# A two-layer attention kernel: in the first layer the inverted row sums reach the channels by two transfers through memory, and the turn of the maxima moves between the two projections

## The chip, the cores and the metric

One core of a Trainium2 chip runs the kernel. The metric is the device time of one execution in microseconds (us). A difference of under 1% of it is taken as no change.

## The reference

The input x is 32 images of 16 x 16 tokens with 256 channels. Two layers follow one another, each a residual around attention on the group-normalised input (`_gn`: 32 groups of 8 channels, statistics per image).

```
x = x + _L0_conv_ref(_gn(x), ...)      # windowed cosine attention, shifted windows of 8 x 8
x = x + _L1_conv_ref(_gn(x), ...)      # masked attention, 8 heads look back and 8 look ahead
```

The change is in the first layer alone. There an image is rolled by (-4, -4) and cut into 4 windows of 64 tokens; with 16 heads of 16 channels:

```
qn = q / max(|q|, 1e-12);  kn = k / max(|k|, 1e-12)
logits = qn @ kn^T * exp(min(logit_scale, log 100)) + 16 * sigmoid(bias)   # masked across the roll
scores = softmax(logits, axis=-1)                                          # 64 keys per query
o = scores @ v;   z = o @ Wo^T + bo                                        # back to 256 channels
```

The softmax divides by a sum for each head and each query. The kernel weighs the values first and divides the 256 channels of the result afterwards, so each inverted sum is needed in the 16 rows (channels) of its head.

## The kernel before, in words

**Layout.** In the first layer channels lie on the 128 partitions in 2 tiles (`o`), tokens along the free axis: 256 for an image. Scores lie with keys of two heads on 2 x 64 partitions, and 4 quarters (`r`, QUADS) in 4 PSUM banks, `psG`. Sums go to `psE`, four quarters of 32 rows each. `psA` has three banks: two for the projections of queries and keys, one for the values and the weighed values.

**Order of the work.** Each engine runs its own list of stages, written out by hand, in `pipeline`: in step s every stage of the list runs for image s + lag, in the order of the list. Steps -6 to 3 and 26 to 32 are written out, the steps between are a loop of two steps in a pass. Engines meet only at semaphores (`wait`), and each engine's list is executed in order. `wait_alone` is a wait followed by a `nop` inside the loop.

**TensorE's step** (list at L467): `scores` of image s (L339, L346), `project_v` of s+1 (L382), `output` of s-1 (L396), `bounds` of s+1 (L363, L370), `turn` of s+2 (L407), `sums` of s (L417), `weigh` of s (L431), `project` half 0 of s+3 (L443), `groups` of s+4 (L458), `project` half 1 of s+3 (L443 again), `turn_c` of s+1 (L450), and `spread_sums` of s (L465): one 128 x 128 by 128 x 512 product in float32, recorded as two matmuls, that copies each inverted sum into the 16 rows of its head. `output` waits for the divided heads, `scores` for the turned maxima (`c_out`), `turn` for the unit queries and keys (`qkn_done`), `sums` for both halves of `add_bias`.

**VectorE's step** (list at L740): `add_bias` half 0 (L634), `unit_qk` (L714, two), `add_bias` half 1, `take_max` (L707, two), `invert_sums` (L618), `spread_blocks` (L623), `stats_next` (L722), `stats_first` (L729 to L737), `variances` (L647 to L653), `norms` (L641, twice, each after one `square`), `outputs` (L613), `seeds` (L663 to L669) and `roots` (L675 to L699). `spread_blocks` writes the inverse sums, masked by block, as a 128 x 512 operand `rdx` for `spread_sums`; `outputs` multiplies the result in `psE` with the weighed values in `ot`.

**ScalarE's step** (list at L565): the two halves of `exponent` (L522), `copy_v`, `copy_z`, `normalize`, `copy_qk`, `copy_o` (L547, fills `ot`), `square` half 0 and half 1 (L506), and `copy_c` (L552), which turns the maxima in `psG` into the bfloat16 operand that `scores` of the next step uses.

**GpSimd** adds the residual. **SyncE** has one stage in the loop, `load` (L286): the 256 KB image s+6 into `X`, once the statistics of image s+4 are done.

The second layer is not touched.

Of the kernel before, what the change touches and what calls it, by code (L numbers as in the profile page):

```python
# [30 lines left out]
P = 128  # L31
# [149 lines left out]
def layer0(nc, ctx, images, xr, given, X, stats2, probs, xh, stack, ident, gavg, A, G, E):  # L181
    def sb(name, shape, dt=F32):
        return ctx.enter_context(nc.sbuf_tensor(name, shape, dt))

    def sem(name):
        return ctx.enter_context(nc.semaphore(name))
# [5 lines left out]
    qkn = probs[0][:, 3072:4096].rearrange("p (t c) -> p t c", t=TT)  # L192
    rdx = probs[0][:, 4096:4608]
    sel = probs[0][:, 4608:4864].rearrange("p (n j) -> p n j", j=COL)
    spread = probs[0][:, 4864:4992]
    aqf = probs[0][:, 4992:5248]
    zb = probs[1][:, 2048:2560].rearrange("p (c t) -> p c t", c=CT)
    wo = probs[1][:, 3072:3584].rearrange("p (c o) -> p c o", c=CT)
# [30 lines left out]
    own = sb("own0", [P, 2])  # L229
    half_of = sb("half_of", [P, 2])  # L230
    slot_of = sb("slot_of", [P, 4])
    block_of = sb("block_of", [P, 8])
    group_of = sb("group_of", [P, QUADS, 2])
    region_keys = sb("region_keys", [P, 4, WTOK], BF16)
    region_queries = sb("region_queries", [P, TOKENS], BF16)
    pick = sb("pick0", [P, 4, WTOK], BF16)
# [2 lines left out]


    x_in = [sem(f"x_in{k}") for k in range(2)]
    pv_done, proj_qk, proj_v, max_ready, s_ready, z_ready, turned, c_turned, g_ready, spread_done = (
        sem(n) for n in ("pv_done", "proj_qk", "proj_v", "max_ready", "s_ready", "z_ready", "turned",
                         "c_turned", "g_ready", "spread_done"))
    squared, exp_done, z_out, qk_out, c_out, xh_done, v_out = (
        sem(n) for n in ("squared", "exp_done", "z_out", "qk_out", "c_out", "xh_done", "v_out"))
    r_done, o_done, sum_done, gn_chain, rs_ready, max_done, qkn_done, x1_done, stats = (
        sem(n) for n in ("r_done", "o_done", "sum_done", "gn_chain", "rs_ready", "max_done", "qkn_done",
                         "x1_done", "stats"))
    newton, biased, rdx_done, sums_done, o_out = (sem(n) for n in ("newton", "biased", "rdx_done", "sums_done", "o_out"))  # L250
    LAGS = (-1, 6)
    NEWTON = 9
    CUBIC = math.sqrt(0.375)
# [14 lines left out]
           (scale, given["scale0"]), (bv, given["bv0"]), (bo, given["bo0"]), (wo, given["wo0"])]  # L268
    others = [(gavg, given["gavg"]), (wqk, given["wqk0"]), (ident, given["ident"]), (wv, given["wv0"])]
    REGIONS = 2 * QUADS  # L270
    MADE = 12
    TABLE_STEP = -2

    with nc.Block() as block:
        @block.sync
        def _(sp):
            for group, done in ((net, c_net), (others, c_in)):
                for dst, src in group:
                    sp.dma_start(dst if isinstance(dst, bass.AP) else dst[:], src).then_inc(done, 16)
            sp.wait_ge(z_in, 2)  # L280
            for r in range(QUADS):
                rows = slice(r * COL + SLOTS, r * COL + SLOTS + MASKS)
                sp.dma_start(region_keys[rows, :, :], given["aux"][0:MASKS, 1, 0:4, win(WINDOWS - 1)]).then_inc(region_in, 16)
                sp.dma_start(region_queries[rows, :], given["aux"][0:MASKS, 0, 0, :]).then_inc(region_in, 16)

            def load(i):  # L286

                wait_alone(sp, stats, i.plus(-2).count(4, 1))
                src = xr.rearrange("(c p) i t -> p c i t", p=P)[:, :, bass.ds(i.index(), 1), :]
                sp.dma_start(X[:, bass.ds(i.index(1), 1), :, :].rearrange("p i c t -> p c (i t)"),  # L290
                             src.rearrange("p c i t -> p c (i t)")).then_inc(x_in[i.k], 16)

            pipeline(sp, images, [(load, 6)], LAGS)

        @block.tensor
        def _(pe):
# [114 lines left out]
            def sums(i):  # L411

                wait(pe, biased, i.count(2))
                wait(pe, z_out, i.plus(-1).count(2))
                for n in range(8):
                    for r in range(QUADS):
                        last = nc.tensor.matmul(E[own_rows(r), 0:WTOK], sel[:, n, :], prob[i.k][:, r, n // WINDOWS, n % WINDOWS, :],  # L417
                                                start=(n == 0), stop=(n == 7), tile_position=(0, r * COL), skip_group_check=True)
                        if n == 7:
                            last.then_inc(sums_done, 1)  # L420
# [38 lines left out]
                                 bn[i.k][:, :, :].rearrange("p c (h s) -> p (c h) s", s=3)[:, :, 1:3],  # L459
                                 start=True, stop=True).then_inc(g_ready, 1)  # L460

            def spread_sums(i):

                wait(pe, rdx_done, i.count(1))
                nc.tensor.matmul(E[:, :], spread, rdx, start=True, stop=True).then_inc(spread_done, 1)  # L465

            pipeline(pe, images, [(scores, 0), (project_v, 1), (output, -1), (bounds, 1), (turn, 2), (sums, 0), (weigh, 0),  # L467
                                  (lambda i: project(i, 0), 3), (groups, 4), (lambda i: project(i, 1), 3), (turn_c, 1),
                                  (spread_sums, 0)], LAGS, once=(TABLE_STEP, prepare))

        @block.scalar
        def _(act):
# [81 lines left out]
            def normalize(i):  # L554
# [3 lines left out]
                for c in range(CT):  # L558
                    src = X[:, bass.ds(i.index(1), 1), c, :].rearrange("p i (t rr ww c) -> p (i t) rr ww c", t=TT, rr=WIN, ww=2)
                    dst = xh[i.k][:, c, :].rearrange("p (t ww rr c) -> p t rr ww c", t=TT, ww=2, rr=WIN)  # L560
                    for ww in range(2):
# [2 lines left out]

            pipeline(act, images, [(lambda i: exponent(i, 0), 0), (lambda i: exponent(i, 1), 0),  # L565
                                   (copy_v, 1), (copy_z, -1), (normalize, 3), (copy_qk, 2),
                                   (copy_o, 0), (lambda i: square(i, 0), 3), (lambda i: square(i, 1), 3), (copy_c, 1)], LAGS, once=(TABLE_STEP, finish_table))

        @block.vector
        def _(dve):  # L570
# [7 lines left out]
            def prepare():  # L578
                dve.wait_ge(c_in, 16 * len(others))
                dve.wait_ge(region_in, 16 * REGIONS)  # L580
                nc.vector.tensor_scalar(aqf, region_queries[:, :], -1.0, None, ALU.mult).then_inc(made, 1)
                unit = ident[:, :]
                nc.vector.reduce_sum(own[:, :], unit.rearrange("p (r e d) -> p e r d", e=2, d=DIM), AX_XY).then_inc(summed, 1)
                nc.vector.reduce_sum(half_of[:, :], unit.rearrange("p (e k) -> p e k", e=2), AX_X).then_inc(summed, 1)
                nc.vector.reduce_sum(slot_of[:, :], unit.rearrange("p (r j) -> p j r", j=COL)[:, 0:SLOTS, :],
                                     AX_X).then_inc(summed, 1)
                by_sum = unit.rearrange("p (r u e n) -> p u r e n", r=QUADS, u=2, e=2)[:, 0]
                nc.vector.reduce_sum(block_of[:, :], by_sum.rearrange("p r e n -> p n r e"), AX_XY).then_inc(summed, 1)
                nc.vector.reduce_sum(group_of[:, :, :], by_sum, AX_X).then_inc(summed, 1)
                dve.wait_ge(summed, 5)  # L590
                nc.vector.tensor_tensor(pick[:, :, :], region_keys[:, :, :], slot_of[:, :].unsqueeze(2).to_broadcast([P, SLOTS, WTOK]),
                                        ALU.add).then_inc(made, 1)
                nc.vector.tensor_copy(spread.rearrange("p (g d) -> p g d", d=DIM),
                                      group_of[:, :, :].rearrange("p r e -> p (r e)").unsqueeze(2)
                                      .to_broadcast([P, 8, DIM])).then_inc(made, 1)
                for n in range(8):
                    nc.vector.tensor_copy(sel[:, n, :].rearrange("p (u e n) -> p u e n", u=2, e=2)[:, :, :, n],
                                          half_of[:, :].unsqueeze(1).to_broadcast([P, 2, 2])).then_inc(made, 1)
                dve.wait_ge(p_cm, 1)
                nc.vector.tensor_copy(cm[:, :, :].rearrange("p t s -> p (t s)"), G[:, 512:768]).then_inc(made, 1)  # L600
                dve.wait_ge(made, MADE)

                dve.wait_ge(a_tab, 1)
                nc.vector.tensor_scalar(table, table, 1.0, None, ALU.add).then_inc(d_tab, 1)
                dve.wait_ge(d_tab, 1)
                nc.vector.reciprocal(table, table).then_inc(d_tab, 1)

            def outputs(i):

                wait(dve, spread_done, i.count(1))  # L610
                wait(dve, o_out, i.count(1))
                raw = ot[:, :, :].rearrange("p o t -> p (o t)")
                nc.vector.tensor_tensor(raw, E[:, :], raw, ALU.mult).then_inc(o_done, 1)  # L613

            def invert_sums(i):
                wait(dve, sums_done, i.count(QUADS))
                wait(dve, rdx_done, i.plus(-1).count(1))
                nc.vector.reciprocal(rd[:, :], E[:, 0:WTOK]).then_inc(r_done, 1)  # L618

            def spread_blocks(i):  # L620
                wait(dve, r_done, i.count(1))
                wait(dve, spread_done, i.plus(-1).count(1))
                nc.vector.tensor_tensor(rdx.rearrange("p (n q) -> p n q", q=WTOK), rd[:, :].unsqueeze(1).to_broadcast([P, 8, WTOK]),  # L623
                                        block_of[:, :].unsqueeze(2).to_broadcast([P, 8, WTOK]), ALU.mult).then_inc(rdx_done, 1)

            def add_bias(i, part):

# [97 lines left out]
            def stats_first(i):  # L725
                wait_alone(dve, x_in[i.k], i.dmas(1))
                wait_alone(dve, g_ready, i.plus(-2).count(1))
                for c in range(CT):
# [9 lines left out]
                                               op0=ALU.mult, op1=ALU.add).then_inc(stats, 1)  # L738

            pipeline(dve, images, [(lambda i: add_bias(i, 0), 0), (unit_qk, 2), (lambda i: add_bias(i, 1), 0), (lambda i: take_max(i, 0), 1), (lambda i: take_max(i, 1), 1),  # L740
                                   (invert_sums, 0), (spread_blocks, 0), (stats_next, -1), (stats_first, 5),
                                   (variances, 4), (lambda i: norms(i, 0), 3), (lambda i: norms(i, 1), 3), (outputs, 0),
                                   (seeds, 4, 1), (roots, 4, 1)], LAGS,
                     once=(TABLE_STEP, prepare))
# [544 lines left out]
```

## Time and profile before

| | |
|---|---|
| time, median of 3 runs | 1286.02 us (1282.92 to 1295.72) |
| the profiled execution's own time | 1287.98 us |
| its span | 1286.3 us |
| TensorE's granted clock, mean over the span | 0.975 |
| first layer, from the span's start to about | 565 us |
| TensorE matmuls busy | 1194.4 us (93%) |
| TensorE weight loads busy | 864.1 us (67%) |
| VectorE busy | 897.7 us (70%) |
| ScalarE busy | 610.9 us (47%) |
| GpSimd busy | 207.4 us (16%) |

How to read it: the times of the engines overlap, so they don't add up to the span. A busy share is an average over both layers; what one instruction is worth is read from the step in which it runs. The profile's span is 1.7 us shorter than the execution's time, and the execution is 2 us above the median of the runs.

### The profile page before, as it was taken

Reading aid. Unit: us, or ns where it says so; the run is one execution under the profiler, and the core shown is the slowest. Engines: PE = TensorE matmul, PEld = TensorE weight load, DVE = VectorE, ACT = ScalarE, POOL = GpSimd, SP = SyncE. Lnnn points to the kernel's source line nnn. Section 1 sums busy time; section 2 is a strip of 40 time slices with the busy share of each in tenths; the row PEclk is TensorE's granted clock in tenths of the full one; section 3 lists DMA queues with packets and bytes.
Section 4 is the critical chain, followed back from the end, with each engine's and each line's share of the span. In section 5 each row is a group of like instructions: output and inputs, shape, how many; then the busy total and the mean of one; then the engine's idle time right before and its main releaser. Section 6 shows DMA issues by size and latency. Waiting matters only on the chain.

```text
span 1286.3 us, 50697 instructions
## 1 busy us (share of the span) xinstructions
PE 1194.4 (93%) x21404; PEld 864.1 (67%) x21404; DVE 897.7 (70%) x1591; ACT 610.9 (47%) x1019; POOL 207.4 (16%) x271
## 2 busy tenths in 40 slices
PE   6789999999999999958999999999999999999983
PEld 2567777777677677736677776767777777767652
DVE  1488898798888888645576666767666666767643
ACT  2355565555555555512444444444444444445430
POOL 0001111111111111121222212212222212222120
PEclk9699999999999999989999999999999999999987
DMA  2000000000000000010232423333232323333233
GB/s 80 13 20 20 20 17 17 20 16 25 12 24 16 18 12 3 5 38 1 34 65 64 79 48 74 52 70 57 65 58 66 75 51 76 51 71 56 67 58 74
DMA packets 304632, 54.35 MB, mean 42 GB/s; under 512 B 270724, under 2 KB 303766, under 8 KB 304534
## 3 DMA queue, kind: packets, MB, share of 16 engines
q1 hardware_dynamic: 303480, 52.75, 19.9%
q8 instruction: 83, 1.36, 0.4%
q10 hardware_dynamic: 1056, 0.13, 0.1%
q14 instruction: 13, 0.11, 0.0%
HBM read 27.56 MB, written 25.17 MB: 41 GB/s over the span
## 4 chain that ended last, share of the span: by engine, by line
PE 45%; DVE 5%; issue 3%; ACT 1%; DMA 1%; SPq 0%; POOL 0%; POOLq 0%; DVEq 0%
PE psG L979 8%; PE psA L1042 7%; PE psG L1011 6%; PE psA L1056 5%; PE psG L1022 5%; PE psE L1090 5%; PE psA L1068 4%; DVE of L1189 3%; PE psG L994 2%; DVE sums L1184 2%; PE psE L1080 1%; ACT probs L1113 0%; SPq L947 0%; DVE cm L1165 0%; DMA scratch_heads<-ots 0%
## 5 line engine op out<-in xcount | busy, mean ns | idle before, releaser
L1165 DVE TENSOR_REDUCE cm<-psG 128x4 f32<-128x1024 f32 (+1 forms) x192 | 235.2, 1225 | 174.5 <-PE psG L1022 174.3
L1113 ACT ACTIVATE probs<-psG 128x1024 f32<-128x1024 f32 x192 | 196.5, 1023 | 240.5 <-PE psG L994 240.5
L1219 POOL TENSOR_SCALAR_AFFINE_SELECT probs<-probs 128x1024 f32<-128x1024 f32 x128 | 139.1, 1098 | 551.0 <-ACT probs L1113 551.0
L979 PE MATMUL psG<-stack 32*128 32x512 f32 (+1 forms) x1024 | 219.2, 525 | 6.3 <-ACT probs L1113 6.3
L1011 PE MATMUL psG<-stack 32*128 32x256 f32 (+1 forms) x2048 | 219.2, 341 | 4.1 <-DVE cm L1165 2.7
L1011 PEld LDWEIGHTS psG<-stack 32*128 32x128 f32 x2048 | 149.6, 185 | 10.8 <-DVE cm L1165 3.4
L764 POOL TENSOR_TENSOR X<-X,probs 128x96 f32 (+5 forms) x128 | 62.0, 515 | 499.2 <-ACT probs L529 499.2
L443 PE MATMUL psA<-probs,xh 128*128 128x512 f32 x256 | 130.5, 637 | 9.3 <-ACT xh L562 5.3
L1056 PE MATMUL psA<-xh,wqk 128*128 128x256 f32 x512 | 122.6, 383 | 5.7 <-DVE xh L1195 5.7
L979 PEld LDWEIGHTS psG<-stack 32*128 32x128 f32 x1024 | 82.8, 185 | 61.6 <-issue 54.3
L1184 DVE RECIPROCAL sums<-sums 128x128 f32<-128x128 f32 x128 | 115.7, 929 | 12.0 <-DMA sums<-scratch_heads 12.0
L1056 PEld LDWEIGHTS psA<-xh,wqk 128*128 128x128 f32 x512 | 93.3, 192 | 17.4 <-DVE xh L1195 6.4
L1042 PE MATMUL psA<-probs,va 128*32 128x256 f32 (+1 forms) x2048 | 97.8, 332 | 0.9 <-POOL probs L1219 0.9
L522 ACT ACTIVATE probs<-psG 128x1024 f32<-128x1024 f32 x64 | 62.0, 1021 | 76.1 <-PE psG L346 76.1
L634 DVE TENSOR_TENSOR probs<-probs,ebias 128x1024 f32<-128x1024 f32 x64 | 77.9, 1219 | 14.6 <-ACT probs L522 14.5
L1090 PE MATMUL psE<-of,wo 128*128 128x256 f32 x256 | 67.0, 407 | 21.7 <-DVE of L1189 20.5
L707 DVE TENSOR_REDUCE cm<-psG 128x16 f32<-128x1024 f32 x64 | 75.4, 1219 | 14.8 <-PE psG L370 13.9
L1042 PEld LDWEIGHTS psA<-probs,va 128*32 128x32 f32 x2048 | 57.8, 110 | 34.5 <-issue 11.7
L506 ACT ACTIVATE probs<-psA 128x512 f32<-128x512 f32 x64 | 38.2, 597 | 87.1 <-PE psA L443 83.0
L443 PEld LDWEIGHTS psA<-probs,xh 128*128 128x128 f32 x256 | 45.6, 198 | 45.6 <-issue 33.2
L994 PE MATMUL psG<-ct,pick 32*128 32x256 bf16 (+1 forms) x1024 | 74.4, 242 | 0.0
L1090 PEld LDWEIGHTS psE<-of,wo 128*128 128x128 f32 x256 | 48.2, 198 | 36.2 <-DVE of L1189 23.2
(132 smaller groups left out, 1925.5 us busy)
## 6 DMA issues: line engine op xcount, KB each, us to landing
scratch_heads<-ots SPq DMA_DIRECT2D x256, 64.0 KB, 3.6
X<-in_xr SPq DMA_DIRECT2D x32, 256.0 KB, 2.8
raw<-scratch_heads SPq DMA_DIRECT2D x32, 256.0 KB, 2.7
sums<-scratch_heads SPq DMA_DIRECT2D x32, 256.0 KB, 3.0
out<-X SPq DMA_DIRECT2D x32, 256.0 KB, 2.9
probs<-in_wqk SPq DMA_DIRECT2D x1, 512.0 KB, 4.0
wv<-in_wv SPq DMA_DIRECT2D x2, 256.0 KB, 4.2
wqk<-in_wqk SPq DMA_DIRECT2D x1, 512.0 KB, 4.0
```

What stands on the lines that cost most here:

```text
L443: last = nc.tensor.matmul(A[t][:], xh[i.k][:, c, t * P:(t + 1) * P], wqk[:, c, :], start=(c == 0), stop=(c == CT - 1))
L634: nc.vector.tensor_tensor(both, both, bias.unsqueeze(2).to_broadcast([P, 4, WINDOWS, WTOK]), ALU.mult).then_inc(biased, 1)
L979: nc.tensor.matmul(G[:, at:at + 2 * b.size].rearrange("p (e q) -> p e q", e=2), kt[i.k][own_rows(r), o, b.keys_of(o) * P:(b.keys_of(o) + 1 ...
L994: last = nc.tensor.matmul(G[:, at:at + b.size], pick[own_rows(r), e, :], ct[o][own_rows(r), b.queries(o)], start=False, stop=True, skip_gr ...
L1011: nc.tensor.matmul(G[:, at:at + b.size], qm[i.k][own_rows(r), o, e, b.queries_of(o) * P:(b.queries_of(o) + 1) * P], kt[i.k][own_rows(r), o ...
L1042: last = nc.tensor.matmul(A[0 if o else 2][COL * c:COL * (c + 1), to:to + b.size], va[i.k][:, b.keys_of(o), TILE_HEADS * o + 2 * r + e, :] ...
L1056: last = nc.tensor.matmul(A[o][:, n * TOKENS:(n + 1) * TOKENS], wqk[:, c, n * CH + o * P:n * CH + (o + 1) * P], xh[i.k][:, c, :], start=(c ...
L1090: last = nc.tensor.matmul(E[:, o * TOKENS:(o + 1) * TOKENS], wo[:, f, o * P:(o + 1) * P], of[:, f, :], start=(f == 0), stop=(f == CT - 1))
L1113: nc.scalar.activation(weights[:, b.weights_at:b.weights_at + 1024], G[:, 0:1024], ACT.Exp).then_inc(exp_done, 1)
L1165: nc.vector.reduce_max(slots, scores, AX_X).then_inc(max_done, 1)
L1184: nc.vector.reciprocal(piece, piece).then_inc(r_done, 1)
L1219: nc.gpsimd.affine_select(out=diagonal, in_=diagonal, compare_op=ALU.is_ge, fill=0.0, base=0, pattern=[[0, QUADS], [0, 2], [sign, P]], cha ...
```

## The change

`spread_sums`, `spread_blocks` and the two reductions and the copy that made their masks (`block_of`, `group_of`, `spread`) are gone. SyncE gets two stages after `load`: `put_inverses` writes the 128 x 64 inverses (32 KB) to one of two buffers in device memory, and `get_inverses`, once that transfer has landed, reads 8 rows of 512 numbers (2 KB) from there, each 16 times, into the 128 x 512 operand `rdx` (256 KB). `outputs` waits for this transfer and multiplies by `rdx` in place of `psE`. The order of the columns in `sel` is changed so that the wanted sums lie where `get_inverses` reads them. `invert_sums` waits for the previous `put`, and `sums` for the previous `invert_sums`. On TensorE `turn_c` moves ahead of the second half of `project`, on ScalarE `copy_c` ahead of the second `square`.

```diff
-    spread = probs[0][:, 4864:4992]
...
-    block_of = sb("block_of", [P, 8])
-    group_of = sb("group_of", [P, QUADS, 2])
+    inverses = nc.dram_tensor("inverses", [2, P, WTOK], F32).ap()
...
-            pipeline(sp, images, [(load, 6)], LAGS)
+            def put_inverses(i):
+                wait_alone(sp, r_done, i.count(1))
+                wait_alone(sp, got[i.k], i.plus(-2).dmas(1))
+                sp.dma_start(inverses[i.k], rd[:, :]).then_inc(put[i.k], 16)
+
+            def get_inverses(i):
+                wait_alone(sp, put[i.k], i.dmas(1))
+                wait_alone(sp, o_done, i.plus(-1).count(1))
+                by_head = inverses[i.k].rearrange("(g u n) q -> g u (n q)", u=2, n=8)[:, 0]
+                sp.dma_start(rdx, by_head.unsqueeze(1).to_broadcast([8, DIM, 512])).then_inc(got[i.k], 16)
+
+            pipeline(sp, images, [(load, 6), (put_inverses, 0), (get_inverses, 0)], LAGS)
...
                 wait(pe, z_out, i.plus(-1).count(2))
+                wait(pe, r_done, i.plus(-1).count(1))
...
-            def spread_sums(i):
-
-                wait(pe, rdx_done, i.count(1))
-                nc.tensor.matmul(E[:, :], spread, rdx, start=True, stop=True).then_inc(spread_done, 1)
-
...
-                                  (lambda i: project(i, 0), 3), (groups, 4), (lambda i: project(i, 1), 3), (turn_c, 1),
-                                  (spread_sums, 0)], LAGS, once=(TABLE_STEP, prepare))
+                                  (lambda i: project(i, 0), 3), (groups, 4), (turn_c, 1), (lambda i: project(i, 1), 3)], LAGS, once=(TABLE_STEP, prepare))
...
-                                   (copy_o, 0), (lambda i: square(i, 0), 3), (lambda i: square(i, 1), 3), (copy_c, 1)], LAGS, once=(TABLE_STEP, finish_table))
+                                   (copy_o, 0), (lambda i: square(i, 0), 3), (copy_c, 1), (lambda i: square(i, 1), 3)], LAGS, once=(TABLE_STEP, finish_table))
...
-                    nc.vector.tensor_copy(sel[:, n, :].rearrange("p (u e n) -> p u e n", u=2, e=2)[:, :, :, n],
+                    nc.vector.tensor_copy(sel[:, n, :].rearrange("p (e u n) -> p u e n", u=2, e=2)[:, :, :, n],
...
-                wait(dve, spread_done, i.count(1))
+                wait_alone(dve, got[i.k], i.dmas(1))
                 wait(dve, o_out, i.count(1))
                 raw = ot[:, :, :].rearrange("p o t -> p (o t)")
-                nc.vector.tensor_tensor(raw, E[:, :], raw, ALU.mult).then_inc(o_done, 1)
+                nc.vector.tensor_tensor(raw, rdx, raw, ALU.mult).then_inc(o_done, 1)

             def invert_sums(i):
                 wait(dve, sums_done, i.count(QUADS))
-                wait(dve, rdx_done, i.plus(-1).count(1))
+                wait_alone(dve, put[1 - i.k], i.plus(-1).dmas(1))
                 nc.vector.reciprocal(rd[:, :], E[:, 0:WTOK]).then_inc(r_done, 1)
-
-            def spread_blocks(i):
-                wait(dve, r_done, i.count(1))
-                wait(dve, spread_done, i.plus(-1).count(1))
-                nc.vector.tensor_tensor(rdx.rearrange("p (n q) -> p n q", q=WTOK), rd[:, :].unsqueeze(1).to_broadcast([P, 8, WTOK]),
-                                        block_of[:, :].unsqueeze(2).to_broadcast([P, 8, WTOK]), ALU.mult).then_inc(rdx_done, 1)
```

## Rows read from the trace of the kernel before

**Rows 1.** Busy time by stretch: start:end, length, engines, granted clock, DMA share, GB/s.
```profile
300.00:400.00 100.00, 96.74 (x2677) 71.73 (x2674) 86.23 (x207) 58.41 (x110) 12.78 (x28) 1.00 0.07 20
```

**Rows 2.** Timeline of one step on PE: start, length, line, operation, count.
```profile
305.85 0.38 PE L450 MATMUL psG<-ident,cm 128*128 128x128 f32 x2
306.06 1.02 PE L465 MATMUL psE<-probs 128*128 128x512 f32 x2
307.05 1.53 PE L339 MATMUL psG<-stack 32*64 32x64 f32 x124
...
314.02 1.09 PE L407 MATMUL psA<-ident,probs 128*128 128x128 f32 x8
315.04 1.10 PE L417 MATMUL psE<-probs 128*32 128x64 f32 x64
...
318.93 1.96 PE L443 MATMUL psA<-probs,xh 128*128 128x512 f32 x4
```

**Rows 3.** Timeline of the same stretch on ACT and DVE; idle time before in brackets.
```profile
306.05 0.60 ACT L506 ACTIVATE probs<-psA 128x512 f32<-128x512 f32 x1 [1.34 <-DVE rs L641]
306.68 0.69 DVE L641 TENSOR_REDUCE rs<-probs 128x32 f32<-128x512 f32 x1 [0.62 <-ACT probs L506]
307.28 0.68 DVE L613 TENSOR_TENSOR ot<-psE,ot 128x512 f32<-128x512 f32 x1
...
310.62 1.22 DVE L634 TENSOR_TENSOR probs<-probs,ebias 128x1024 f32<-128x1024 f32 x1
311.75 1.28 DVE L714 TENSOR_TENSOR probs<-psA,rs_y 128x512 f32<-128x512 f32 x2
312.95 1.22 DVE L634 TENSOR_TENSOR probs<-probs,ebias 128x1024 f32<-128x1024 f32 x1
314.26 2.36 DVE L707 TENSOR_REDUCE cm<-psG 128x16 f32<-128x1024 f32 x2
316.53 0.55 DVE L618 RECIPROCAL rd<-psE 128x64 f32<-128x64 f32 x1
317.12 0.69 DVE L623 TENSOR_TENSOR probs<-rd,block_of 128x512 f32<-128x512 f32 x1
317.73 0.75 DVE L722 BATCH_NORM_STATS2 stats<-X  x2
```

**Rows 4.** Timeline on PE: first and last of 28 steps, L465 in each.
```profile
88.56 1.02 PE L465 MATMUL psE<-probs 128*128 128x512 f32 x2
...
508.34 1.02 PE L465 MATMUL psE<-probs 128*128 128x512 f32 x2
```

**Rows 5.** DMA issues of the page: size, us from issue to landing (medians).
```profile
X<-in_xr SPq DMA_DIRECT2D x32, 256.0 KB, 2.8
...
out<-X SPq DMA_DIRECT2D x32, 256.0 KB, 2.9
```

**Rows 6.** DMA queue q1: packets, MB, share of 16 engines; the whole span, then 100 to 560 us.
```profile
q1 hardware_dynamic: 303480, 52.75, 19.9%
```
```profile
q1 hardware_dynamic: 6528, 6.29, 4.6%
```

**Rows 7.** The chain that ended last, in time: start, length, what.
```profile
1267.78 3.64 DMA scratch_heads<-ots
1271.42 0.02 issue
1271.44 0.36 SPq L955
```

**Rows 8.** The last steps of the first layer, timeline on DVE, then PE.
```profile
547.62 0.55 DVE L618 RECIPROCAL rd<-psE 128x64 f32<-128x64 f32 x1
...
556.78 0.56 DVE L618 RECIPROCAL rd<-psE 128x64 f32<-128x64 f32 x1 [1.30 <-PE psE L417]
...
559.28 0.69 DVE L613 TENSOR_TENSOR ot<-psE,ot 128x512 f32<-128x512 f32 x1 [0.56 <-PE psE L465]
```
```profile
551.90 2.05 PE L396 MATMUL psE<-ot,probs 128*128 128x128 f32 x16
...
555.53 1.10 PE L417 MATMUL psE<-probs 128*32 128x64 f32 x64 [1.58 <-DVE probs L634]
```

**Rows 9.** Busy time by stretch: around a long wait of PE inside `scores`.
```profile
228.00:231.00 3.00, 1.33 (x115) 1.19 (x110) 2.57 (x13) 0.00 (x0) 0.00 (x0) 1.00 0.00 0
231.00:236.00 5.00, 5.00 (x70) 4.47 (x49) 3.44 (x4) 3.12 (x4) 0.00 (x0) 0.66 0.01 3
```

More of the change, by code:

```diff
@@ L241, in layer0 @@
     x_in = [sem(f"x_in{k}") for k in range(2)]
[L242 removed]
+    pv_done, proj_qk, proj_v, max_ready, s_ready, z_ready, turned, c_turned, g_ready = (
         sem(n) for n in ("pv_done", "proj_qk", "proj_v", "max_ready", "s_ready", "z_ready", "turned",
[L244 removed]
+                         "c_turned", "g_ready"))
     squared, exp_done, z_out, qk_out, c_out, xh_done, v_out = (
@@ L249, in layer0 @@
                          "x1_done", "stats"))
-    newton, biased, rdx_done, sums_done, o_out = (sem(n) for n in ("newton", "biased", "rdx_done", "sums_done", "o_out"))
+    newton, biased, sums_done, o_out = (sem(n) for n in ("newton", "biased", "sums_done", "o_out"))
+    put, got = ([sem(f"{n}{k}") for k in range(2)] for n in ("put", "got"))
     LAGS = (-1, 6)
@@ L270, in layer0 @@
     REGIONS = 2 * QUADS
-    MADE = 12
+    MADE = 11
     TABLE_STEP = -2
@@ L586, in prepare @@
                                      AX_X).then_inc(summed, 1)
[L587 to L590, printed above, removed]
+                dve.wait_ge(summed, 3)
                 nc.vector.tensor_tensor(pick[:, :, :], region_keys[:, :, :], slot_of[:, :].unsqueeze(2).to_broadcast([P, SLOTS, WTOK]),
                                         ALU.add).then_inc(made, 1)
-                nc.vector.tensor_copy(spread.rearrange("p (g d) -> p g d", d=DIM),
-                                      group_of[:, :, :].rearrange("p r e -> p (r e)").unsqueeze(2)
-                                      .to_broadcast([P, 8, DIM])).then_inc(made, 1)
                 for n in range(8):
-                    nc.vector.tensor_copy(sel[:, n, :].rearrange("p (u e n) -> p u e n", u=2, e=2)[:, :, :, n],
+                    nc.vector.tensor_copy(sel[:, n, :].rearrange("p (e u n) -> p u e n", u=2, e=2)[:, :, :, n],
                                           half_of[:, :].unsqueeze(1).to_broadcast([P, 2, 2])).then_inc(made, 1)
@@ L740, in _ @@
             pipeline(dve, images, [(lambda i: add_bias(i, 0), 0), (unit_qk, 2), (lambda i: add_bias(i, 1), 0), (lambda i: take_max(i, 0), 1), (lambda i: take_max(i, 1), 1),
-                                   (invert_sums, 0), (spread_blocks, 0), (stats_next, -1), (stats_first, 5),
+                                   (invert_sums, 0), (stats_next, -1), (stats_first, 5),
                                    (variances, 4), (lambda i: norms(i, 0), 3), (lambda i: norms(i, 1), 3), (outputs, 0),
```

## The prediction

> **What bounds the kernel now.** I read the busy times by stretch first, to see which engine sets the first layer's pace. Between 300 and 400 us TensorE is busy 97% of the time at full clock and VectorE 86% [rows 1]: TensorE leads, VectorE is close behind. Then I read the timeline of one step, engine by engine. On TensorE there is no gap; `spread_sums` starts at 306.06 and `scores` of the next step at 307.05, so it takes 0.99 us of the step [rows 2]. On VectorE the only gap is 0.62 us before the second `norms`, which waits for the second `square`, and that for the second `project` [rows 3]. VectorE then has 7.5 us of work without a pause up to the end of `add_bias`. The 28 steps from 88.56 to 508.34 us take 419.78 us [rows 4]. 17 of their 27 gaps are 14.86 to 15.03 us, 14.93 on average; ten are longer because TensorE's sequencer stalls: 16.46, 15.45, 16.26, 18.76, 16.18, 17.30, 16.22, 17.39, 16.49 and 15.53, together 166.04.
>
> **The change part by part.** The sum is made against the profiled execution, 1288 us, 2 us above the median.
>
> *Removed on TensorE*: 0.99 us in each step. TensorE's own step would be 14.93 - 0.99 = 13.94 us. *Removed on VectorE*: `spread_blocks`, from 317.12 to 317.73, 0.6 us [rows 3]. The masks are made once, by three small instructions before the first step; I count nothing.
>
> *Moved*: `turn_c` costs 0.21 us (305.85 to 306.06) [rows 2] wherever it stands, and `groups` ahead of it already waits for both maxima, so it waits for nothing new. It makes the second `project`, and so the second `square`, 0.21 us later. In return `copy_c` runs under the second `project`, and `scores` can start at once. Its cover before was `spread_sums`.
>
> *The chain across the engines, if the transfers are hidden.* The second `project` ends at 306.01 (`square` starts at 306.05). `norms`, `outputs`, `seeds`, `roots`, `add_bias`, `unit_qk` and `add_bias` follow without a gap to 312.95 + 1.22 = 314.17, 8.16 us later [rows 3]. Before, `sums` started at 315.04 only because TensorE was busy. TensorE alone would now reach `sums` 7.99 us after the start of `scores` (307.05 to 315.04), or 7.8 us after the end of `project`, as pitches overlap by 0.16. So VectorE becomes what `sums` waits for: 8.16 + 0.04 for the semaphore. From `sums` to the end of the next second `project` it is 318.93 - 315.04 + 0.21 + 1.96 = 6.06 us [rows 2]. The step cannot be shorter than 14.26 us: of the 0.99 us only 0.67 can be had.
>
> *Added: the transfers.* `outputs` now waits for `rdx`, in VectorE's list, and behind it stand `seeds`, `roots`, `add_bias` and `unit_qk`, for which `turn`, `sums` and `normalize` wait. Call L the time from the end of the reciprocal to the start of `outputs`. The ring on VectorE is: end of `add_bias` (314.17) to the end of the reciprocal (316.53 + 0.55), 2.91; L; start of `outputs` to end of `add_bias` (307.28 to 314.17), 6.89 [rows 3]. Step = 9.80 + L. It is hidden up to L = 4.46, and equals today's 14.93 at L = 5.13.
>
> No row has these two transfers. A 256 KB image in 256 packets of 1 KB lands in 2.8 us, a 256 KB store in 2.9 [rows 5]. Between 100 and 560 us 24 image loads took 4.6% of 16 engines [rows 6]: 0.88 us on each engine for one load, 55 ns a packet. Over the whole span a packet has 174 bytes and takes 13.5 ns [rows 6]. The line through both is about 5 ns + 0.049 ns a byte (an estimate): 18 ns for a packet of 256 bytes, 105 ns for one of 2 KB. The `put` (128 packets of 256 bytes) takes 0.14 us on each engine, so 2.8 - 0.74 = 2.1 us; bounds 1.4 us (the same step again below it, for a store that is quick on a quiet queue) and 2.9 (the store as it stands). I take 2.1, the size taken off the nearest row. The `get` (128 packets of 2 KB) takes 0.84 us on each of 16 engines, then it lands in 2.8; if it runs on half of them 1.68, then in 3.6. Its source has an outer count of 8 (8 rows, each read 16 times) where the image's is 128, so it is likelier near the upper end; but 105 ns is a line drawn beyond its points, and larger packets may be cheaper. I take 3.3.
>
> The Trainium skill, "DMA: Bandwidth & Descriptors", section "Why a DMA increments its semaphore by 16 and not by 1", says that the number of engines is the largest up to 16 that divides the outermost count of both patterns. That would be 8 here, and L 0.3 us longer than I take; no row of before shows it.
>
> Handing over costs little: from landing to the next issue 0.02 us [rows 7]. With the register work and `nop` of `wait_alone` I take 0.05 + 0.1 + 0.05. L = 0.05 + 2.1 + 0.1 + 3.3 + 0.05 = 5.6, bounds 4.4 and 6.7. SyncE's queue: `load` of the next image is issued just behind the `get`, so it does not delay it, and lands a step before it is used. `sums` waits for a reciprocal a step old, `invert_sums` for a `put` long landed: nothing.
>
> *The sum.* Step = 9.80 + 5.6 = 15.40. The 17 even steps: 17 x (15.40 - 14.93) = +8.0. In the ten long ones TensorE's stall covers the ring, and they become the larger of 15.40 and the old one less 0.99: 15.47, 15.40, 15.40, 17.77, 15.40, 16.31, 15.40, 16.40, 15.50, 15.40 = 158.45, so -7.6. The layer's end has no work to cover L. For the last image the reciprocal ends at 557.34 and `outputs` starts at 559.28 [rows 8]: 1.94 becomes 5.6, +3.7. For the one before, 548.17 + 5.6 + 0.69 + 2.05 (`output`) = 556.5, and `sums`, queued behind it, stood at 555.53 [rows 8]: +1.0. Total +5.1: 1293 for the execution, **1291 us** against the median.
>
> **The rivals.**
>
> *A. The transfers become the bound (slower).* The place is `outputs` on VectorE. At put 2.9 and get 3.6, L = 6.7, step 16.50: +26.7, +0.2, and +6.9 at the end: +34, 1320. It costs over 13 us from L = 5.9 on (15.70: +13.1 - 5.7 + 5.3). For it: a `get` on half of the engines and `put` as taken give just this 5.9, +13, 1299. Against it: everything else on the queue is idle at that time.
>
> *B. The transfers are nearly hidden (faster).* `get` as an image load, 2.8, put 2.0: L = 5.0, step 14.80: -2.2 - 9.3 + 3.5 = -8, 1278. With L at 4.4 the chain across the engines holds, 14.26: -11.4 - 9.9 + 2.5 = -19, 1267. For it: equal bytes to the image's. Against it: the 8 rows, and two landings in a row need under 4.75 us for a gain of 1%.
>
> *C. The removed matmul was not what TensorE waited for.* It covered the sequencer's fetches at the loop's head; stalls appear in its place. TensorE has about 1.4 us of idle time in a step by then (15.40 - 13.94), which hides them: 1286 to 1293, within 1%.
>
> *D. The clock.* TensorE waits before `turn` and `sums`, these 1.4 us a step. After a wait of 1.67 us inside `scores` the granted clock fell to 0.66 of full speed for 5 us [rows 9], that is partly the lower of its two levels (1.2 GHz); that step took 18.76 us, and one with a like stall and no fall 17.30. If this came in every second step, 1.46 x 14 = 20 us, less what the wait on VectorE absorbs, some half: 1301. Against it: the step with 17.30 lies in the stretch that shows 1.00 [rows 1].
>
> **How the numbers follow.** Under 1%, 13 us, is what a measurement of this kernel can't tell from no change. Chances: forecast (L 5.1 to 5.9) 0.42, its own range 1281 to 1299; A beyond 5.9 0.27; B 0.23; C 0.03; D 0.05. Of B 0.19 is beyond -13 us, since the bounds of `put` are wide to the low side. Faster 0.19, within 1% 0.49, slower 0.32. The range leaves out the outer part of A and B: 1267 to 1310.
>
> **What would show it.** Right: no L465 and no L623; `outputs` on VectorE with idle time before it ended by the DMA of `rdx`, 1 us a step; `turn` on TensorE released by L714; even steps of 15.4 us, so longer than 14.93 although 1 us of TensorE's work is gone; `put` landing in about 2.1 and `get` in about 3.3 us; `scores` with no wait for `copy_c`. Wrong: a `get` at 2.8 or a put under 1.7 (steps below 14.9); landings above 6 us together; a granted clock under 1.00 in the even steps; long steps that don't shorten.

## The result, and the profile after

The changed kernel takes 1325.9 us (median of 4 runs, 1319.65 to 1328.93) against 1284.5 before: 1.032 times as long, 95% interval 1.026 to 1.038. The forecast was 1291, its range ended at 1310. The profiled execution took 1323.1 us, its span is 1321.3, 35.0 longer than before.

**Where it went.** From the first layer's last `output` to the end of the span it is 724 us before and 725 after. In the first layer, the 28 steps that took 419.8 us [rows 4] now take 443.2 between starts of `turn_c`, +23.4. From there to the end of the last `output` it is 12.4 us longer, and the start is 1.7 shorter. The median gap is 16.04 us; counted in the same way it was 14.98. TensorE's timeline, the first and last of 28:

```profile
86.66 0.42 PE L461 MATMUL psG<-ident,cm 128*128 128x128 f32 x2
...
529.88 0.41 PE L461 MATMUL psG<-ident,cm 128*128 128x128 f32 x2
```

One step of the changed kernel: VectorE, then SyncE's queue, then TensorE (start, length, line, operation, count, idle time before and what ended it). It answers to [rows 2, 3].

```profile
330.05 0.54 DVE L617 RECIPROCAL rd<-psE 128x64 f32<-128x64 f32 x1
...
334.60 0.69 DVE L634 TENSOR_REDUCE rs<-probs 128x32 f32<-128x512 f32 x1 [1.26 <-ACT probs L511]
336.48 0.69 DVE L612 TENSOR_TENSOR ot<-probs,ot 128x512 f32<-128x512 f32 x1 [1.19 <-DMA probs<-inverses]
```
```profile
330.73 0.35 SPq L295 DMA_DIRECT2D inverses<-rd  x1
332.33 0.62 SPq L301 DMA_DIRECT2D probs<-inverses  x1
333.67 0.39 SPq L289 DMA_DIRECT2D X<-in_xr  x1
```
```profile
342.71 1.09 PE L417 MATMUL psA<-ident,probs 128*128 128x128 f32 x8 [1.80 <-DVE probs L707]
```

Read it as the ring of the prediction. The reciprocal ends at 330.59. The `put` is issued 0.14 later, the `get` 1.60 after the `put`, and `outputs` starts 4.15 after the `get` was issued: L = 5.89 us here. In the loop's other steps it is 5.9 to 6.5, median 6.2, but for one of 9.14; the prediction took 5.6. VectorE is idle for 1.19 us, and TensorE, which had no gap before, waits 1.80 us before `turn` for the unit queries and keys. 9.80 + 6.2 = 16.0 us is the step.

The page's DMA issues (size, us from issue to landing; the `get` has no figure) answer to [rows 5]. The image's load, now issued behind the `get`, lands later too; no engine is seen to wait for it:

```profile
X<-in_xr SPq DMA_DIRECT2D x32, 256.0 KB, 3.5
...
inverses<-rd SPq DMA_DIRECT2D x32, 32.0 KB, 1.5
```

From the issue of the `get` to the start of `outputs` it is 4.4 us in the median of the loop's steps (4.1 to 4.7). The layer's last six `get`s have no image's load behind them and stand outside the loop, without the `nop` of `wait_alone`; there it is 3.8 to 4.1. The prediction held that the load does not delay the `get`. What of the difference is the load's, no run separates.

**The clock** falls after some of TensorE's waits: here after the one before `turn`, whose 8 transposes then take 1.64 us in place of 1.09 and `sums` 1.93 in place of 1.10. Five of the 27 steps have such a fall, 17.5 to 17.9 us long, each with a short one behind it; the ten together are 3.6 us longer than ten medians. And it falls in the last steps, where TensorE waits for VectorE and that for the `get`. TensorE's timeline first:

```profile
310.25 1.64 PE L417 MATMUL psA<-ident,probs 128*128 128x128 f32 x8 [1.91 <-DVE probs L707]
311.82 1.93 PE L428 MATMUL psE<-probs 128*32 128x64 f32 x64
...
579.26 3.78 PE L406 MATMUL psE<-ot,probs 128*128 128x128 f32 x16 [3.38 <-DVE ot L612]
584.02 1.10 PE L428 MATMUL psE<-probs 128*32 128x64 f32 x64 [0.97 <-issue]
592.40 3.79 PE L406 MATMUL psE<-ot,probs 128*128 128x128 f32 x16 [6.39 <-DVE ot L612]
```

The granted clock in both places (start:end, length, PE, PEld, DVE, ACT, POOL busy, clock as a share of 2.4 GHz, DMA share, GB/s):

```profile
310.20:316.90 6.70, 6.65 (x144) 5.27 (x145) 5.63 (x10) 2.56 (x5) 1.32 (x2) 0.75 0.02 5
...
572.00:580.00 8.00, 2.94 (x148) 2.46 (x148) 1.49 (x2) 2.60 (x4) 0.00 (x0) 0.81 0.15 42
580.00:586.00 6.00, 5.03 (x143) 4.61 (x141) 2.24 (x4) 0.84 (x2) 1.70 (x4) 0.69 0.01 3
586.00:597.00 11.00, 3.79 (x18) 3.49 (x16) 1.17 (x3) 1.37 (x3) 0.00 (x0) 0.71 0.09 27
```

Most of the 12.4 us of the layer's end, in rows: `output` takes 3.78 and 3.79 us where it took 2.05 [rows 8], +3.5 for the two. And the `outputs` before each wait for L, as does the one before them (4.69 us):

```profile
578.51 0.69 DVE L612 TENSOR_TENSOR ot<-probs,ot 128x512 f32<-128x512 f32 x1 [6.54 <-DMA probs<-inverses]
585.23 0.56 DVE L617 RECIPROCAL rd<-psE 128x64 f32<-128x64 f32 x1 [3.76 <-PE psE L428]
591.66 0.69 DVE L612 TENSOR_TENSOR ot<-probs,ot 128x512 f32<-128x512 f32 x1 [5.18 <-DMA probs<-inverses]
```

For the last image it is 591.66 - 585.79 = 5.87 us where it was 1.94 [rows 8].

### The profile page after: what moved, and what is told of

The parts are those of the page before. It is cut to its first block, busy times and chain, and to the rows that moved or that the text cites. A ratio compares the mean times of both kernels' runs of the same rounds, so it can differ in the third digit from the quotient of the medians.

```text
span 1321.3 us, 50738 instructions
## 1 busy us (share of the span) xinstructions
PE 1181.3 (89%) x21340; PEld 865.4 (65%) x21340; DVE 877.8 (66%) x1556; ACT 613.7 (46%) x1019; POOL 235.9 (18%) x271
## 4 chain that ended last, share of the span: by engine, by line
PE 44%; DVE 5%; issue 3%; ACT 1%; DMA 1%; SPq 0%; POOL 0%; POOLq 0%; DVEq 0%
PE psG L972 8%; PE psA L1035 7%; PE psG L1004 6%; PE psA L1049 5%; PE psG L1015 5%; PE psE L1083 5%; PE psA L1061 4%; DVE of L1182 2%; PE psG L987 2%; DVE sums L1177 2%; PE psE L1073 1%; ACT probs L1106 0%; SPq L940 0%; DVE cm L1158 0%; DMA scratch_heads<-ots 0%
## 5 line engine op out<-in xcount | busy, mean ns | idle before, releaser
L757 POOL TENSOR_TENSOR X<-X,probs 128x96 f32 (+5 forms) x128 | 90.5, 736 | 504.9 <-ACT probs L534 504.9
L1177 DVE RECIPROCAL sums<-sums 128x128 f32<-128x128 f32 x128 | 115.7, 929 | 12.1 <-DMA sums<-scratch_heads 12.1
L1049 PEld LDWEIGHTS psA<-xh,wqk 128*128 128x128 f32 x512 | 93.8, 194 | 17.5 <-DVE xh L1188 6.4
L406 PE MATMUL psE<-ot,probs 128*128 128x128 f32 x512 | 69.1, 291 | 10.5 <-DVE ot L612 10.3
L417 PE MATMUL psA<-ident,probs 128*128 128x128 f32 x256 | 37.9, 295 | 44.7 <-DVE probs L707 44.7
```

What stands on the lines that cost most here:

```text
L757: nc.gpsimd.tensor_tensor(part(new, rd_, cd), part(old, r0, c0), part(zb[:, :, :], r0, c0), ALU.add).then_inc(x1_done, 1)
L1049: last = nc.tensor.matmul(A[o][:, n * TOKENS:(n + 1) * TOKENS], wqk[:, c, n * CH + o * P:n * CH + (o + 1) * P], xh[i.k][:, c, :], start=(c ...
L1177: nc.vector.reciprocal(piece, piece).then_inc(r_done, 1)
```

## The experiments

Each was run beside the kernel before on its chip; ratios are to that kernel, with 95% intervals. Steps are medians of the 27 gaps between starts of `turn_c`. Diffs of the stage lists show only the stages that move.

**1. The same `get` over all engines.** The rows of `inverses` hold every sum twice (u = 0 and 1). Read both and the source's outer count is 16, with the same bytes, packets and result.

```diff
-                by_head = inverses[i.k].rearrange("(g u n) q -> g u (n q)", u=2, n=8)[:, 0]
-                sp.dma_start(rdx, by_head.unsqueeze(1).to_broadcast([8, DIM, 512])).then_inc(got[i.k], 16)
+                by_half = inverses[i.k].rearrange("(g n) q -> g (n q)", n=8)
+                sp.dma_start(rdx, by_half.unsqueeze(1).to_broadcast([16, 8, 512])).then_inc(got[i.k], 16)
```


> Theory 1: VectorE's ring through the transfers is the bound (step = 9.80 + L), and the get is slow, 4.2 us, because its source's outer count of 8 puts it on half of the DMA engines. Here the source is the same data with an outer count of 16 (both copies of each head's sums), same bytes, same 2 KB packets, same result. The get falls to about 3.1 us, L from 6.1 to about 5.0, even steps from 16.0 to about 14.9 us, and the time by some 25 us to about 1298, ratio to before 1.01. Rival: the get is slow for another reason (the read right behind a write, the broadcast, the size of the packets): it stays at 4.2 us and the time at 1325, ratio 1.03.

Measured: 1.0033 (1.0001 to 1.0065), steps 15.08 us. The page shows the `get` at 3.3 us:

```profile
probs<-inverses SPq DMA_DIRECT2D x32, 256.0 KB, 3.3
```
```profile
245.78 0.69 DVE L612 TENSOR_TENSOR ot<-probs,ot 128x512 f32<-128x512 f32 x1 [0.71 <-DMA probs<-inverses]
```

The first line is the page's, the second a step on VectorE, whose wait is shorter. From issue to use the `get` takes 3.4 us in the median in place of 4.4. L is mostly 4.9 to 5.6, and 9.80 + 5.15 = 14.95, within 0.13 of the step. This is the second point on the line step = 9.80 + L. One number in an access pattern is worth most of the loss: 1.032, or 1.025 on this run's chip (experiment 6), becomes 1.003.

The windows show what the outer count does. The layer's last `get` has the queue for itself; here are slices of 0.4 us out of it, from the changed kernel and then from this run (as above: next to last, the mean busy share of the 16 DMA engines):

```profile
589.40:589.80 0.40, 0.00 (x0) 0.00 (x0) 0.00 (x0) 0.00 (x0) 0.00 (x0) 1.00 0.53 205
589.80:590.20 0.40, 0.00 (x0) 0.00 (x0) 0.00 (x0) 0.00 (x0) 0.00 (x0) 1.00 0.57 200
```
```profile
554.00:554.40 0.40, 0.00 (x0) 0.00 (x0) 0.00 (x0) 0.00 (x0) 0.00 (x0) 0.58 0.96 317
```

About half of the engines' time is used with 8 rows and nearly all with 16. That fits the rule of the Trainium skill ("DMA: Bandwidth & Descriptors", section "Why a DMA increments its semaphore by 16 and not by 1") on the number of engines.

**2. The moves alone**, in the kernel before.

```diff
-  (lambda i: project(i, 1), 3), (turn_c, 1), (spread_sums, 0)]      # TensorE
+  (turn_c, 1), (lambda i: project(i, 1), 3), (spread_sums, 0)]
-  (lambda i: square(i, 1), 3), (copy_c, 1)]                         # ScalarE
+  (copy_c, 1), (lambda i: square(i, 1), 3)]
```


> The kernel before with only the two moves (turn_c ahead of the second project, copy_c ahead of the second square). Theory 1: no wait is added or taken away, the second square comes 0.21 us later and finds VectorE with slack before sums: ratio 1.00, steps 14.9 us. Rival: the move itself is part of the loss, since the second norms come later in a ring that is already tight: steps 15.1 us, ratio 1.005 or more.

Measured: 0.9995 (0.996 to 1.0029), steps 14.81. The moves are no part of the loss.

**3. No transfers.** Both stages are taken from SyncE's list, with the waits for them on VectorE; `rdx` is filled once.

```diff
-            pipeline(sp, images, [(load, 6), (put_inverses, 0), (get_inverses, 0)], LAGS)
+            pipeline(sp, images, [(load, 6)], LAGS)
-                wait_alone(dve, got[i.k], i.dmas(1))
-                wait_alone(dve, put[1 - i.k], i.plus(-1).dmas(1))
+            nc.gpsimd.memset(rdx, 0.5).then_inc(z_in, 1)
```


> The changed kernel with neither transfer: outputs multiplies by a constant operand and waits for no transfer, so the division by the row sums is left out. Theory 1: this is the floor that the change could have reached. The chain second project, square, norms, outputs, seeds, roots, add_bias, unit_qk, add_bias, sums holds the step at 14.26 us, not TensorE's own 13.94: 27 steps give about 18 us, ratio 0.985. Rival: TensorE alone is the bound once the matmul is gone: steps of 13.94 us, ratio 0.977. Second rival: the matmul was never what counted and stalls of the sequencer take its place: ratio 1.00.

Measured: 0.9873 (0.9825 to 0.9921). So the two transfers, as they stand, cost 3.8 to 4.5% (1.025, on this run's chip, or 1.032 over 0.987). The steps are 14.73 us and not 14.26: theory 1 was right in its bound (in experiment 4 shorter work on VectorE shortens the step) and 0.47 us short in its size. VectorE's timeline shows why: the second `add_bias` takes 1.70 us here, while it took 1.22 [rows 3], and GpSimd runs at that time. In the step before it takes 1.31, and VectorE pauses for 0.32 us ("issue") at the loop's head.

```profile
244.44 1.70 DVE L625 TENSOR_TENSOR probs<-probs,ebias 128x1024 f32<-128x1024 f32 x1
```
```profile
244.27 0.79 POOL L756 TENSOR_TENSOR X<-X,probs 128x288 f32 x1 [12.04 <-ACT probs L534]
```

**4. No transfers, and GpSimd kept apart** (`add_bias` first, then `residual`).

```diff
                 wait(pool, z_out, i.count(2))
+                if i.plus(1).among(images):
+                    wait(pool, biased, i.plus(1).count(2))
```


> The changed kernel without transfers (outputs multiplies by a constant, so the division by the row sums is left out), and with GpSimd's residual held back until both add_bias of its step are done. Theory: the step without transfers is 14.72 us and not 14.26 because the residual now runs beside the second add_bias, which takes 1.31 or 1.70 us in place of 1.22, while GpSimd's pieces take 0.66 in place of 0.51 us; apart, add_bias takes 1.22 again and the step 14.4 to 14.5 us, 6 to 8 us less in all, ratio 0.982. Rival: the longer add_bias has another cause (a pause of the sequencer at the loop's head, TensorE's reads): it stays at 1.3 to 1.7 us, ratio 0.987 or more.

Measured: 0.985 (0.977 to 0.993), which alone does not tell it from 0.987. The trace does. Steps alternate between 14.23 and 14.64 us. Groups by line between 100 and 480 us (busy us, mean ns of one), first without the new wait, then with it:

```profile
L625 DVE TENSOR_TENSOR probs<-probs,ebias 128x1024 f32<-128x1024 f32 x50 | 65.9, 1318 | 7.6 <-ACT probs L527 5.0 <-issue 2.6
L756 POOL TENSOR_TENSOR X<-X,probs 128x288 f32 (+3 forms) x100 | 63.1, 660 | 316.0 <-ACT probs L534 316.0
```
```profile
L625 DVE TENSOR_TENSOR probs<-probs,ebias 128x1024 f32<-128x1024 f32 x52 | 63.3, 1218 | 5.4 <-issue 2.9 <-ACT probs L527 2.5
L758 POOL TENSOR_TENSOR X<-X,probs 128x288 f32 (+3 forms) x102 | 43.8, 461 | 336.8 <-DVE probs L625 320.8 <-ACT probs L534 16.0
```

Both engines slow each other when they run on SBUF at once: 1318 against 1218 ns, 660 against 461. (The Trainium skill, "Advanced Engine Details and Errata", section "VectorE Performance Modes", says that VectorE's second SBUF port is shared with GpSimd and expects the two to get in each other's way where VectorE uses both ports in a performance mode. Its table gives `tensor_tensor` no such mode; the trace shows the slowdown for it all the same.) The 14.64 of every second step is near the predicted 14.26 with the pause of 0.32 us on VectorE added. In the mean of two steps the collision costs 0.29 us (14.72 against 14.43).

**5. The old places, with transfers.** `turn_c` and `copy_c` go back in the changed kernel (the edit of experiment 2, reversed).

> The changed kernel with turn_c and copy_c back in their old places (behind the second project and the second square). Theory 1 (VectorE's ring through the transfers bounds the step, about 16.0 us): TensorE has over a microsecond of idle time, so that copy_c, now uncovered ahead of scores, is paid from it: same time as the changed kernel, ratio 1.03. Rival: the turned maxima are on the path once the matmul is gone: steps 0.3 to 0.6 us longer, ratio 1.04.

Measured: 1.0288 (1.0218 to 1.0358), steps 16.07. `scores` now waits for `copy_c`, and the wait before `turn` is shorter in exchange. TensorE's timeline of one step:

```profile
236.09 1.53 PE L349 MATMUL psG<-stack 32*64 32x64 f32 x124 [0.92 <-ACT ct L557]
...
244.35 1.09 PE L417 MATMUL psA<-ident,probs 128*128 128x128 f32 x8 [1.22 <-DVE probs L707]
```

**6. A matmul put back, where TensorE waits.** Into the changed kernel, and for comparison into the kernel before:

```diff
+            def filler(i):
+                wait(pe, v_out, i.count(2))
+                nc.tensor.matmul(A[2][:], ident[:, :], wqk[:, 0, :], start=True, stop=True)
-  (bounds, 1), (turn, 2), (sums, 0)
+  (bounds, 1), (filler, 1), (turn, 2), (sums, 0)
```


> The changed kernel with a matmul of the removed one's size (128 x 128 by 128 x 512, float32, 0.99 us) put back between bounds and turn, with a result that nobody reads. Theory 1: TensorE waits 1.6 to 2.1 us before turn in each step, so the matmul costs nothing: ratio 1.03 as without it; where the granted clock fell in that wait (4 of 27 steps) it stays up, which may give back 2 to 5 us. Rival: TensorE is still the bound and the loss is extra work or stalls on it: 27 more microseconds, ratio 1.05.

Measured: 1.0484 (1.0411 to 1.0557), 16 thousandths or 21 us above the changed kernel's first ratio. By the time alone this is the rival (1.05) and not theory 1. The steps speak against the rival: their median is 16.24 us, 0.20 and not 0.99 above the changed kernel's, and TensorE's stalls are 30.9 us in place of 13.2. So it was run again beside the changed kernel and the kernel before with the same edit.

> The changed kernel once more, beside the next two on one chip: ratio 1.03. Even steps 16.0 us, put 1.5 us. Where TensorE's sequencer stalls (fetches at the loop's head), the put issued in the same microseconds lands late, 3 to 5 us, if fetch and transfer share what they wait for; otherwise the late puts and the stalls fall on different steps.

> The changed kernel with the extra matmul of 0.99 us before turn, again, beside the changed kernel. Theory 1, amended: even steps stay at 16.0 to 16.2 us (TensorE is not the bound), but TensorE's wait absorbed about 1 us of each sequencer stall, which it now cannot: ratio up to 0.01 above the changed kernel's. Rival (TensorE bounds): even steps 17 us, 0.02 or more above it. Third: the 0.016 of the first run was mostly its chip and its number of stalls, then there is no difference here.

> The kernel before with the same extra matmul of 0.99 us between bounds and turn. There TensorE is the bound: every step is 0.97 to 0.99 us longer (15.9), 32 steps give 31 us, ratio 1.024. If TensorE were not the bound before, less. It tells what 0.99 us of TensorE's work is worth in a kernel where it counts, against what it is worth in the changed one.

Measured: changed kernel 1.0248 (1.0193 to 1.0302), with the matmul 1.035 (1.0273 to 1.0427), the kernel before with the matmul 1.0416 (1.0367 to 1.0465). Theory 1, amended, held (0.010 above the changed kernel), and the kernel before missed its forecast of 1.024.

The steps without a stall tell most. In the kernel before they grow from 14.96 to 15.82 us in the mean, so there TensorE's work counts. In the changed kernel their median is 16.0 without the matmul and 15.7 to 15.9 with it, and TensorE's wait before `turn` shrinks from mostly 1.6 to 2.1 us to 0.2 to 1.0: there the matmul is hidden. In all, 0.99 us of TensorE's work a step costs 52 us where TensorE is the bound and 17 to 21 where the transfers are. About 23 of the 52 (27 x 0.86) are this growth; the rest, and all of the 17 to 21, comes with the steps that have a stall. The sequencer's stalls ("issue" of 0.15 us or more before a matmul, 75 to 560 us) add up to 32.0 us with the matmul and 12.1 without it in the changed kernel, 27.1 and 15.6 in the one before. A stall can cost more than its own length, since the clock may fall in it: in the kernel before the granted clock between 100 and 560 us is 0.97 with the matmul and 1.00 without, and `project_v` behind a stall of 2.09 us takes 3.45 us at a granted clock of 0.60, where it takes 1.97 in a step without one. The kernel before with the matmul, first that `project_v`, then a step without a stall (317.44 to 333.32, 15.88 us):

```profile
157.10 3.45 PE L382 MATMUL psA<-wv,xh 128*64 128x128 f32 x31 [2.09 <-issue]
```
```profile
317.44 1.02 PE L469 MATMUL psE<-probs 128*128 128x512 f32 x2
...
325.49 1.12 PE L403 MATMUL psA<-probs,ident 128*128 128x512 f32 x2
326.45 1.04 PE L411 MATMUL psA<-ident,probs 128*128 128x128 f32 x8
...
333.32 1.02 PE L469 MATMUL psE<-probs 128*128 128x512 f32 x2
```

Why this edit brings more stalls was not settled.

The last of the expectations to be read is on late `put`s. SyncE's queue and TensorE in the changed kernel's longest step (20.51 us):

```profile
362.67 0.35 SPq L295 DMA_DIRECT2D inverses<-rd  x1
367.50 0.62 SPq L301 DMA_DIRECT2D probs<-inverses  x1
```
```profile
368.08 1.33 PE L349 MATMUL psG<-stack 32*64 32x64 f32 x82 [2.20 <-issue]
371.42 0.94 PE L349 MATMUL psG<-stack 32*64 32x64 f32 x41 [2.01 <-issue]
```

From the `put`'s issue to the `get`'s it is 4.83 us in place of 1.60, and TensorE's sequencer stalls at the same time. In the four profiles with the 8-row `get` and no other order (two of the changed kernel, two with the matmul) this is over 3.2 us 11 times before 560 us, and each time a stall of 0.8 us or more follows within 8 us. The other four profiles with transfers have five more: three go with such a stall, and two, of 3.40 us in experiment 1 and 3.52 us in experiment 5, both in the layer's fourth step, do not; in the changed kernel's two profiles that step has 3.02 and 3.08 us, also without one. There are stalls without a late `put`, too. So the long ones, of over 3.6 us, all go with a stall of TensorE's sequencer; which of the two comes first, or whether a third thing holds up both, stays open.

**7. More of VectorE's work over the transfers.** `outputs` goes behind `seeds` and `roots`, `output` behind `bounds`, `copy_z` behind `normalize`; once with the 16-row `get`, once with the 8-row one.

```diff
-  (lambda i: norms(i, 1), 3), (outputs, 0), (seeds, 4, 1), (roots, 4, 1)]      # VectorE
+  (lambda i: norms(i, 1), 3), (seeds, 4, 1), (roots, 4, 1), (outputs, 0)]
-  (project_v, 1), (output, -1), (bounds, 1), (turn, 2)                         # TensorE
+  (project_v, 1), (bounds, 1), (output, -1), (turn, 2)
-  (copy_v, 1), (copy_z, -1), (normalize, 3)                                    # ScalarE
+  (copy_v, 1), (normalize, 3), (copy_z, -1)
```


> The changed kernel with the get of e1 and with outputs behind seeds and roots on VectorE, output behind bounds on TensorE, copy_z behind normalize on ScalarE: 2.7 us of VectorE's work now cover the transfers. Theory 1: L of up to about 7.1 us is hidden, the step falls to about 14.3 us, ratio 0.985 to 0.99 (the layer's end still pays for L). Rival: the wait comes back elsewhere, as sums on TensorE then waits for copy_z (which follows output), or normalize for newton: steps of 15 us or more, ratio 1.00 or above.

> The changed kernel with its own get (8 rows, 4.2 us) and with outputs behind seeds and roots, output behind bounds, copy_z behind normalize. Theory 1: the transfers cost only what VectorE cannot cover; 7.7 us lie between the reciprocal and outputs, L is 6.1, so the step is 14.6 us as with the faster get, ratio 1.00 (a little above it, as the layer's end shows L three times). Rival: the transfers cost something by being there (the image's load behind them, the queue, fetches of instructions), beside VectorE's wait: ratio 1.01 to 1.03.

Measured: 0.997 (0.9934 to 1.0005) and 1.0073 (1.0035 to 1.011), steps 14.62 us in both. Theory 1 of the first missed in size (14.3 us and 0.985 to 0.99 were forecast): VectorE now idles 0.30 us before `seeds`, which need what `norms` has just written, and by the rows that is most of the difference. With the slow `get`, too, VectorE no longer waits between `roots` and `outputs`:

```profile
238.86 0.55 DVE L617 RECIPROCAL rd<-psE 128x64 f32<-128x64 f32 x1
...
244.41 0.23 DVE L656 SCALAR_TENSOR_TENSOR rs<-rs 128x66 f32<-128x66 f32 x1 [0.30 <-DVE rs L634]
...
247.08 0.15 DVE L692 SCALAR_TENSOR_TENSOR shift<-gs,rs_y 128x2 f32<-128x2 f32 x1
247.15 0.69 DVE L612 TENSOR_TENSOR ot<-probs,ot 128x512 f32<-128x512 f32 x1
```

7.74 us lie between the reciprocal and `outputs`; 6.2 of transfers fit in. In the steps without a stall the transfers' whole cost was the wait: a `get` slower by 1.0 us changes nothing. What they still cost is seen at the layer's end, where nothing covers them: from the layer's 28th `turn_c` to the last `outputs` it is 73.6 us with the fast `get`, 79.7 with the slow one, and 66.0 in the kernel before. This is why steps 0.36 us shorter than before end as no measurable gain. The 6.1 us between the two `get`s are about half of what parts the two ratios (0.010 or 13 us); the two ran on different chips. In these steps `add_bias` takes 1.22 us again and GpSimd's pieces 0.46, as with GpSimd kept apart.

## Why the prediction was wrong

**The mechanism held, the size did not.** The bound did pass from TensorE to VectorE's ring through the transfers. Two points lie near the line step = 9.80 + L: 16.04 at 6.2, and 15.08 at 5.15 (experiment 1). With L covered, the step no longer depends on it (experiment 7). The loss was on the forecast's side, but its +5 us meant no change, and +35 was measured between the profiled executions. At its full L of 6.7 rival A stood at 1320, and it was given 0.27 for everything beyond 5.9.

**The first step that failed is the `get`'s size.** "I take 3.3" measured 4.4 with its hand-over, in the loop. The bounds, 2.8 on 16 engines and 3.6 on half, were both too low: the runs have 3.3 and, less 0.1 for the hand-over, 4.3. The `put` was mis-sized the other way, 1.5 for 2.1, and the hand-over from the reciprocal to the `put` was 0.14 to 0.21 for 0.05, so that L came out at 6.2 where 5.6 was taken. The outer count was read rightly and the half-way value then taken; the full 3.6 would have given 1299. The line of 105 ns a packet, the doubt that I had voiced, was not the weak place: the engines' busy time in the layer's last `get` is 0.8 us on each of 16, or 1.6 on half of them (estimates, share times length over the slices of that transfer), where 0.84 and 1.68 were taken. Too low was what stands beside it. It was taken over from the image's load as 2.8 - 0.88 = 1.9 us; for this last `get` it is 3.94 - 1.6 = 2.3 and 3.2 - 0.8 = 2.4 from issue to use. With L = 6.2 the prediction's own rules give +14.6 in the steps and +5.8 at the end, some 20 of the 35 us.

**The second is the long steps.** They were to become 7.6 us shorter in all, "TensorE's stall covers the ring"; at steps of 16.0 the same rule gives 3.6 shorter. The 27 gaps are 8.8 us longer together than by that rule. Two things are seen in them: the falls of the clock above, and stalls that lengthen the ring that they were to cover. In the longest step (20.51 us) the `put` landed late while the sequencer stalled.

**The third is the layer's end**: +4.7 forecast, +12.4 measured, where L = 6.2 explains 5.8. The last three `outputs` wait for the transfers, the late `put` of one brought its L to 7.14 us, and the clock, rival D's matter, fell for the last two `output`s (+3.5). In the steps themselves rival D was small, the 3.6 us above.

**The floor** was worked out as 14.26 and is 14.23 in every second step (experiment 4), but only with GpSimd apart; without transfers and with GpSimd as it is, 14.73. That is a collision which the change sets up by making `output` earlier against VectorE's work, and the prediction did not look at GpSimd. In the changed kernel, too, `add_bias` takes 1.26 us in the mean and GpSimd's pieces 0.77, for 1.22 and 0.51 before. It did not decide this case, since the ring was longer. By the traces it takes 0.29 us of the 0.67 that could be had in a step, and the pause at the loop's head another 0.16 in the mean.

**Rival C** (stalls appear in the matmul's place): not seen, 13.2 us of stalls after and 15.6 before.

## What to carry to other kernels

A matmul of 1 us on the busiest engine is not worth two transfers in series through memory (6 us) unless the waiting engine has that much other work behind which the wait can stand: count the work between the issue and the use, not the busy share. For a transfer that repeats few rows, look at the outermost count of its pattern: here 16 in place of 8 took 1.0 us off each. And where an engine's list is in order, first try to move the waiting stage behind work that doesn't need it: the same slow transfers cost 3% in one place and 0.7% in another, and the faster ones nothing that could be measured. None of the versions that still divide was measurably faster than the kernel before; even without the transfers it was 0.987.

## What the runs showed of the hardware

- A 32 KB store in 128 packets of 256 bytes lands in 1.5 us. A 256 KB read that repeats 8 rows of 2 KB is used 4.4 us after its issue with an image's load behind it, and 3.8 to 4.1 after it at the layer's end; the same bytes from 16 rows are used after 3.4 and land in 3.3, an image of 128 rows in 2.8 [rows 5].
- The read from 8 rows shows a DMA share of 0.53 to 0.57 of the 16 engines, the one from 16 rows 0.96.
- VectorE and GpSimd working on SBUF at the same time slow each other: 1.22 to 1.70 us at most on VectorE, 0.46 to 0.66 us in the mean on GpSimd.
- A small transfer on SyncE's queue can land about 3 us late while TensorE's sequencer stalls: 14 of the 16 `put`s over 3.2 us had a stall of 0.8 us or more within 8 us.
